# Order of work on ScalarE and VectorE in the slot loop of a state-space layer: second decay tile, output sums, silus of x and B

## What is computed

```python
proj = hidden_states @ in_proj_w.T                 # gate, x, B, C and dt
xc = conv_general_dilated(xc, conv_w, ...) + conv_b  # causal, 4 taps, per channel
hBC = silu(...)                                    # x, B, C
Lmat = exp(segment_sum(A * dt))                    # decay, 128 x 128 for each chunk and head
M = (C @ B.T) * Lmat;  Y_diag = M @ (x * dt)
Y_off = ...                                        # what the first chunk of a sequence gives the second
y = Y_diag + Y_off + D * x
y = y * rsqrt(mean(y ** 2) + EPS) * norm_w * silu(gate)
out = y @ out_proj_w.T
```

## Time and profile before

| | |
|---|---|
| median of 3 runs | 2211.35 us (2210.16 to 2213.11) |
| the profiled execution | 2212.06 us, span 2210.3 us |
| TensorE busy | 2095.4 us (95%), 12921 matmuls |
| VectorE busy | 1604.6 us (73%) |
| ScalarE busy | 1438.9 us (65%) |
| GpSimd busy | 742.5 us (34%) |
| mean granted TensorE clock | 0.979 |

### The profile page before, as it was taken

One profiled execution on the slowest core, in us unless ns is written; L12 is line 12 of the kernel. 1 busy time (PEld: TensorE's weight loads), 2 busy tenths in 40 slices (PEclk: granted clock), 3 DMA queues, 4 the chain that ended last, 5 costly groups with the idle time before them and its releaser, 6 DMA issues.

```text
span 2210.3 us, 33465 instructions
## 1 busy us (share of the span) xinstructions
PE 2095.4 (95%) x12921; PEld 1677.5 (76%) x12924; DVE 1604.6 (73%) x1697; ACT 1438.9 (65%) x3104; POOL 742.5 (34%) x392
## 2 busy tenths in 40 slices
PE   6799999999999999999999999997799989999998
PEld 5587887887888788788788788874587667777764
DVE  6678877887887878787788878885723457777765
ACT  3676776776777677677677767772633357777761
POOL 2153344444344444344435443534344200000001
PEclk9999999999999999999999999997899999999999
DMA  3121221222122222122122212222032110010001
GB/s 108 73 112 67 96 77 67 105 96 77 67 104 79 70 94 105 67 77 105 67 96 77 105 67 95 78 77 49 30 126 86 48 33 23 17 25 17 18 3 39
DMA packets 49341, 155.84 MB, mean 71 GB/s; under 512 B 13856, under 2 KB 20256, under 8 KB 40736
## 3 DMA queue, kind: packets, MB, share of 16 engines
q1 hardware_dynamic: 49184, 153.70, 20.0%
HBM read 151.06 MB, written 2.62 MB: 70 GB/s over the span
## 4 chain that ended last, share of the span: by engine, by line
PE 84%; DVE 8%; ACT 4%; issue 2%; POOL 2%; DMA 0%; SPq 0%; ACTq 0%; POOLq 0%
PE PS L579 19%; PE PS L581 18%; PE PS L580 18%; PE PS L637 4%; PE PS L801 4%; PE PS L915 3%; PE PS L613 2%; PE PS L899 2%; PE PS L633 2%; PE PS L573 2%; DVE sq L1499 2%; PE PS L922 2%; PE PS L886 2%; PE PS L888 1%; PE PS L887 1%
## 5 line engine op out<-in xcount | busy, mean ns | idle before, releaser
L579 PE MATMUL PS<-xnh,wh 128*128 128x512 f32 x1272 | 515.1, 405 | 28.8 <-DVE sq L1499 17.6
L581 PE MATMUL PS<-xnh,wl 128*128 128x512 f32 x1272 | 502.8, 395 | 0.0
L580 PE MATMUL PS<-xnl,wh 128*128 128x512 f32 x1272 | 501.2, 394 | 0.0
L1461 DVE SCALAR_TENSOR_TENSOR arena<-PS,arena 128x1020 f32<-128x1020 f32 (+2 forms) x240 | 305.6, 1274 | 57.8 <-ACT arena L1119 52.1
L1080 ACT ACTIVATE PS<-x,arena 128x128 f32<-128x128 f32 x1024 | 307.9, 355 | 21.5 <-DVE arena L1493 20.0
L579 PEld LDWEIGHTS PS<-xnh,wh 128*128 128x128 f32 x1272 | 242.8, 191 | 85.7 <-DVE sq L1499 19.3
L581 PEld LDWEIGHTS PS<-xnh,wl 128*128 128x128 f32 x1272 | 242.0, 190 | 53.3
L580 PEld LDWEIGHTS PS<-xnl,wh 128*128 128x128 f32 x1272 | 243.1, 191 | 47.6
L433 POOL TENSOR_TENSOR arena<-arena 128x1024 f32<-128x1024 f32 x64 | 154.9, 2421 | 330.8 <-ACT arena L1098 330.8
L422 POOL TENSOR_TENSOR wl<-arena,wh 128x1024 fp32r<-128x1024 f32 x72 | 184.9, 2568 | 230.1 <-ACT wh L1072 230.1
L437 POOL TENSOR_TENSOR zl<-arena,zh 128x1024 fp32r<-128x1024 f32 x63 | 155.6, 2470 | 302.5 <-ACT zh L1102 302.5
(11 more groups left out here) (223 smaller groups left out, 4119.6 us busy)
## 6 DMA issues: line engine op xcount, KB each, us to landing
x<-decay SPq DMA_DIRECT2D x64, 1024.0 KB, 4.6
arena<-in_w_xg SPq DMA_DIRECT2D x72, 512.0 KB, 5.5
arena<-in_w_o SPq DMA_DIRECT2D x32, 512.0 KB, 3.5
arena<-in_w_f SPq DMA_DIRECT2D x28, 512.0 KB, 3.5
arena<-in_w_h SPq DMA_DIRECT2D x16, 257.0 KB
x<-in_x SPq DMA_DIRECT2D x3, 1024.0 KB, 5.4
out<-x SPq DMA_DIRECT2D x8, 256.0 KB, 2.0
x<-in_x SPq DMA_DIRECT2D x2, 512.0 KB, 4.2
```

The source lines that it names most:

```text
L579: mm(PS[:, bank], ah, bh, start=(n == 0), stop=False)
L580: mm(PS[:, bank], ah, bl, start=False, stop=False)
L581: last = mm(PS[:, bank], al, bh, start=False, stop=(n == len(terms) - 1))
L1461: ins = stt(o, pair_of(bank).rearrange("p q (b t) -> p q b t", t=SEQ)[:, :, :, :SEQ - k], w[:, 3 - k:4 - k], o, ALU.mult, ALU.add)
```

## The change

ScalarE: in every slot the second decay tile is formed ahead of x's constant. In the first two slots the third tile comes ahead of the gate's tanh. The rounding of weights in slots 3 and 4 comes ahead of x's tanh. Ahead of the loop the tanh of C comes ahead of the gate's, the tanh of B ahead of a copy, and one small Tanh is run early, so that the table is there.

VectorE: both output sums come ahead of x's silu; the silu of B comes in slot 5, behind `weigh(t, 0)`, instead of slot 4; the silu of C comes before the sums. In the first two slots the second and third product come one place earlier. TensorE's, GpSimd's and SyncE's lists are unchanged.

```diff
@@ ScalarE, group()
+                    filling = first and i < 2
+                    fall_of(t, k, 1)
                     if n is not None:
                         if t:
                             ac.wait_ge(s["yv"], t + 1)
                         c_x(n, 1 - k)
                     if side in (0, 1):
                         th_bc(g + 1, side)
-                    fall_of(t, k, 1)
+                    if filling:
+                        exp_of(t, k)
                     if n is not None:
                         if t:
                             ac.wait_ge(s["zd"], t)
                         th_g(n, 1 - k)
-                    exp_of(t, k)
+                    if not filling:
+                        exp_of(t, k)
+                    if i in (BCAT - 1, BCAT) and not final:
+                        ac.wait_ge(s["g_ps"], t + 2)
+                        high(x_order(g, i + 1, final) if side == 0 else bc_order(g))
                     if n is not None:
                         ac.wait_ge(s["xs"], t + 1)
                         th_x(n, 1 - k)
-                    if i in (BCAT - 1, BCAT) and not final:
-                        ac.wait_ge(s["g_ps"], t + 2)
-                        high(x_order(g, i + 1, final) if side == 0 else bc_order(g))
@@ ScalarE, ahead of the loop
             act(dtl, dtu, ACT.Ln).then_inc(s["dt_ln"], 1)
+            act(hv[:, 4:5], hv[:, 1:2], ACT.Tanh)
             high(1)
...
             high(2)
+            th_bc(0, 0)
             ac.wait_ge(s["dt_T"], 3)
             act(aT.rearrange("p (q u) h -> p q (u h)", q=2), pair_of(YB), ACT.Copy).then_inc(s["dt_sb"], 1)
             c_x(0, 0)
-            th_bc(0, 0)
+            th_bc(0, 1)
             th_g(0, 0)
-            th_bc(0, 1)
@@ VectorE, group()
                     weigh(t, 0)
+                    if side == 1:
+                        silu_bc(g + 1, 0)
                     if side in (0, 1):
                         conv_bc(g + 1, side, order - 1)
...
                     turned(t)
+                    filling = first and i < 2
+                    if filling:
+                        weigh(t, 1)
                     if n is not None:
                         ve.wait_ge(s["c_x"], t + 2)
                         tap(xs[:, 1 - k], XB, prm[:, n], 1, None, order)
                         tap(xs[:, 1 - k], XB, prm[:, n], 2, None, order)
                         tap(xs[:, 1 - k], XB, prm[:, n], 3, s["conv_x"], order)
-                    weigh(t, 1)
+                    if filling:
+                        weigh(t, 2)
+                    else:
+                        weigh(t, 1)
                     if n is not None:
                         gate(n, 1 - k)
-                    outs = not (first and i < 2)
-                    if outs:
+                    if side == 1:
+                        silu_bc(g + 1, 1)
+                        weigh(t, 2)
+                    if not filling:
                         out_sum(2 * k, XB, 2 * t - 3)
-                    weigh(t, 2)
+                        if side != 1:
+                            weigh(t, 2)
+                        out_sum(2 * k + 1, GB, 2 * t - 2)
                     if n is not None:
                         silu_x(n, 1 - k)
-                    if side in (0, 1):
-                        silu_bc(g + 1, side)
-                    if outs:
-                        out_sum(2 * k + 1, GB, 2 * t - 2)
```

## The result

The changed kernel takes 2239.51 us (median of 4 runs, 2237.26 to 2239.88) against 2210.76 us of the kernel before beside it (4 runs, 2209.09 to 2213.11): ratio 1.0127, 95% interval 1.011 to 1.0145. It is slower by 29 us, where 36 had been forecast (2247 us, range 2224 to 2292). The profiled execution lasted 2239.88 us, its span is 2238.1 us.

What follows compares the result with a forecast made beforehand. TensorE was taken to set the pace. Stalls +68 us, less 31 (output sums) and 14 (start), with slack +19, plus 16 for half clock, on 2212 us, gave 2247 us, range 2224 to 2292.

Steps and rivals of the forecast that it cites:

- The tile ahead of the constant: ScalarE's second decay tile delays taps 2.3 us in 17 even slots, 0.87 in 16 odd, 2.1 in seven slots 6: +68 us.
- slack: Time between x's last tap and TensorE's first output matmul: 0 to 0.2 us, taken as 0.1 over 40 slots.
- The sum of the stalls: TensorE's waits for the taps at the first output matmul, 40 slots: +68 us before slack.
- Output sums and silu of B: Slots 4 and 5: TensorE's 2.5 us wait and half clock go, 0.3 us more; 4.4 us per group, -31 us.
- The start: First slots: TensorE starts 5.0 us earlier, slots 0 and 1 save 5.8 us, full clock 3.3 us; -14 us.
- The dead heat: Odd slots: VectorE's x silu and GpSimd's z_low start together; VectorE taken as first, even delay 2.3 us.
- the rival: GpSimd wins in odd slots, x's silu waits for z_low: even delay 4.2 us, 2288 us; chance 0.27.
- The clock: TensorE drops to half clock after about 60% of the 17 even-slot stalls, 1.6 us each: +16 us.
- The other rivals: Clock hardly falls, 2231 us, chance 0.14; faster, 0.12; no change, near 2212 us, 0.05.
- The faster case: Tile finds idle ScalarE time ahead of x's constant in even slots: 2196 us, or 2167 without any delay; chance 0.12.

Runs made afterwards that it cites:

- the tile alone: Kernel before with only the second decay tile moved ahead of x's constant outside the first two slots: 2296.6 us, ratio 1.0382.
- the start alone: Kernel before with only the early Tanh, the moved tanhs of B and C and the order of slots 0 and 1 changed: 2198.1 us, ratio 0.9938.
- the experiment: Changed kernel with a tiny VectorE memset ahead of x's silu in odd slots, so that GpSimd's z_low is issued first: 2285.3 us, ratio 1.0311.
- x's constant first again: Changed kernel with x's constant again ahead of the second decay tile outside the first two slots: 2163.16 us, ratio 0.9785.
- VectorE's order alone: Kernel before with output sums ahead of x's silu, silu of B in slot 5, silu of C before the sums: 2179.54 us, ratio 0.9852.

## Why the prediction was right, step by step

**The tile ahead of the constant.** Shown by its undoing (-76 us) and by itself (+85 us). The numbers per slot, forecast and measured: taps late in even slots 2.3 and 2.26 us; stall of TensorE 2.2 (2.3 less 0.1 of slack) and 2.06, in odd slots 0.77 and 0.64, in slot 6 2.0 and 2.10. The slack is 0.2 us, the upper of the two bounds. The sum of the stalls was set at 64 us; measured it is 16 x 2.06 + 1.1 + 16 x 0.64 + 7 x 2.10 = 59 us. The 1.1 us is slot 62, which the forecast counted with the rest: the last slots round no more weights, so the tile starts about 1 us sooner.

One term is missing: the matmul behind each waiting one comes 0.1 us later than usual, 4 us over 40 slots.

**Output sums and silu of B.** Forecast -31 us, alone -31.9. That these agree so closely is luck: in the loop the gain is 35 us, 5.0 instead of 4.4 per group, since the wait of 0.4 us for GpSimd's `low` at the start of slot 4 goes too; 4 us of it were lost again behind the loop in that kernel's profiled execution, and are not in the changed kernel's.

**The start.** Forecast -14 us, alone -13.3, again with an offset: 12.3 at slot 2, and the clock of one slot 4. Slot 1's clock gave the 1.3 us that were said (its `outputs` take 1.4 us less), but of the 2.0 us for slot 0's clock only 0.4 came, since the shorter wait of 1.99 us lowers it too. In the changed kernel TensorE's first slot starts 6.5 us sooner instead of 5.0; 1.4 of this is there ahead of the changed part already (the convolutions of B and C start at 49.33 instead of 50.71 us). It is no work of the start's change: the kernel with the tile alone has them at 49.64, the one with the start alone at 50.95.

**The dead heat.** VectorE won, as chosen. What was said for it, that its operands are read early, no run isolates; as an instruction of 0.06 us turned the order in 13 of 15 slots, the right choice was also luck. Slot 6 went to GpSimd, as said. The loss that the rival would have brought is the experiment's: 2285 us where 2288 had been worked out. Z was forecast 1.15 us earlier and came 1.26 (838.13 to 842.24 + 1.60, against 795.08 to 799.18 + 2.87); ScalarE could use 0.8 of it as said, since the squares' end, not z, sets when it goes on. The order of issue decided in both directions: 3.48 us for GpSimd's instruction where VectorE was first, 3.44 for VectorE's where GpSimd was. That is as the Trainium skill, "SBUF — State Buffer", section "Who interferes with whom", has it.

**The clock.** Forecast: 60% of 17 even stalls, +16 us. Measured: it fell behind 9 of the loop's 23 stalls of some 2 us, 6 of 16 in even slots and 3 of 7 in slots 6, which the forecast left out; each is worth eight matmuls x 0.2 = 1.6 us: +14. The share of 60% was too high and the number of stalls too low, so that the sum came out nearly right is in part luck. That the earlier waits lowered it 7 times of 7 was no rule: it was 5 of 7 in the kernel with the tile alone and 6 of 7 in the one with the start alone.

Together, from the traces: the start -14 (12.6 and the 1.4 ahead of it), stalls +59, the matmuls behind them +4, clock +14, sums -35: +28 us, and the span has grown from 2210.3 to 2238.1. Where the first output matmuls of slots 2 and 63 stand shows the parts (us):

| kernel | slot 2 | slot 63 | between | behind slot 63 |
|---|---|---|---|---|
| before | 126.8 | 1484.8 | 1358.0 | 725.5 |
| changed | 114.8 | 1512.9 | 1398.1 | 725.2 |
| x's constant first again | 113.3 | 1436.0 | 1322.8 | 725.1 |
| the tile alone | 130.4 | 1566.7 | 1436.3 | 729.8 |
| VectorE's order alone | 126.4 | 1449.2 | 1322.8 | 729.9 |
| the start alone | 114.5 | 1471.3 | 1356.8 | 724.6 |

The 7.5 us by which the forecast was too high are the difference of terms that go both ways: the base of 2212 (1), stalls (5, of which slack 4 and slot 62 1), clock (2) and output sums (4) make it too high by some 12; the 4 us of the matmuls behind the stalls are missing. The mechanism was right in each part; that the time was so near is also owed to this balance.

**The other rivals.** The faster case began at an even delay under 0.9 us and would have needed idle time ahead of the constant; the trace has none in these slots. The tile is free in the slots that have such idle time; to lose nothing, it would have to go first in these slots alone.

## What to carry to other kernels

A wait that is just met shows in no list of waits: look for instructions that end right when the bounding engine needs them, and follow back what they hang on before putting anything ahead of it. A change of several parts is worth taking apart: two parts here gain 45 us, the third loses 76, and leaving it out gives 2163 us, 2.2% under the kernel before. Where two engines that exclude each other are released by one event, 0.06 us of work decides which waits; don't build on such a margin.

## What was not expected of the hardware

Stalls of equal length lowered TensorE's clock at one time and not at another: 2.06 us at 6 of 16 places, 1.99 us in slot 0 and not in slot 1, 2.5 us in 7 of 7 places of one kernel, 6 of 7 and 5 of 7 of two others. The length of a stall alone does not tell it; what does stays open.
